# A fused attention and expert kernel: normalising later, values one group later, another tail

## The reference, cut to what matters

```
xn = layernorm(x)
q, k = rope(split(xn @ Wq)), rope(split(xn @ Wk));  v = split(xn @ Wv)
sim = where(causal, q @ k.T * 64**-0.5, -inf)
attn = softmax(sim) @ v;  a = merge(attn) @ Wo + bo
probs = softmax(x @ gate_w.T, over rows);  vals, idx = top_k(probs, 8)
merged = sum over the 8 rows of x[idx] * vals
h = gelu([merged, 1] @ w1);  o = [h, 1] @ w2
out = x + a + scatter_add(o * vals)
```

## Time and profile before

| | us |
|---|---|
| median of three runs | 1408.34 |
| lowest and highest | 1407.0, 1410.91 |
| the profiled execution | 1406.38 |
| its span, first to last instruction | 1404.6 |
| PE busy | 1331.6 (95%) |
| POOL busy | 970.3 (69%) |
| DVE busy | 878.1 (63%) |
| ACT busy | 635.2 (45%) |

### The profile page before, as it was taken

The page is one execution under the profiler, slowest core; times in us unless marked ns, Lnnn a source line. Parts: engine busy times, 40 slices in busy tenths (PEclk is TensorE's granted clock), DMA queues, the critical chain, the costliest instruction groups (busy, mean ns, idle before and its releaser), DMA issues.

```text
span 1404.6 us, 31395 instructions
## 1 busy us (share of the span) xinstructions
PE 1331.6 (95%) x11612; PEld 867.7 (62%) x11612; DVE 878.1 (63%) x1202; ACT 635.2 (45%) x963; POOL 970.3 (69%) x661
## 2 busy tenths in 40 slices
PE   6889999999999999999999999999999999999987
PEld 5556566555655555546676776666656776666655
DVE  5797767666565556556347666666666566666633
ACT  3446565453445334524224434444444344554431
POOL 2666688765566656656566777888778668888842
PEclk9999999999999999999999999999999999999999
DMA  5324333669667866665642222212232221212121
GB/s 177 122 84 145 114 134 116 226 211 320 213 230 244 287 215 221 212 235 171 180 137 81 66 75 65 77 62 77 96 102 91 74 76 55 84 62 77 47 58 57
DMA packets 122752, 188.86 MB, mean 134 GB/s; under 512 B 29616, under 2 KB 57808, under 8 KB 122608
## 3 DMA queue, kind: packets, MB, share of 16 engines
q1 hardware_dynamic: 92176, 112.51, 24.4%
q10 hardware_dynamic: 30384, 74.23, 15.4%
q0 software_dynamic: 48, 0.13, 0.1%
HBM read 130.71 MB, written 22.54 MB: 109 GB/s over the span
## 4 chain that ended last, share of the span: by engine, by line
PE 79%; DMA 7%; DVE 5%; issue 4%; ACT 4%; SPq 1%; POOL 0%; ACTq 0%; DVEq 0%; POOLq 0%
PE t_pO L1490 17%; PE t_pF L1465 11%; PE t_pA L1388 9%; PE t_pB L1388 6%; PE t_pF L1448 6%; DMA t_swap<-t_raw 3%; PE t_pA L1412 3%; PE t_pC L1412 3%; PE t_pA L1393 2%; PE t_pC L1499 2%; PE t_pB L1393 2%; PE t_pB L1540 2%; PE t_pC L1540 2%; PE t_pB L1514 1%; ACT t_PT L812 1%
## 5 line engine op out<-in xcount | busy, mean ns | idle before, releaser
L735 POOL TENSOR_TENSOR t_acc<-t_acc,t_PT 128x1024 f32<-128x1024 f32 (+3 forms) x256 | 437.9, 1711 | 161.8 <-ACT t_PT L812 141.6
L710 POOL TENSOR_TENSOR t_swap<-t_swap,t_sin 128x512 f32<-128x512 f32 x124 | 163.8, 1321 | 198.9 <-DMA t_swap<-t_raw 198.3
L1490 PE MATMUL t_pO<-t_PT,t_V 128*64 128x512 f32 (+3 forms) x1536 | 294.1, 504 | 4.7 <-issue 4.7
L812 ACT ACTIVATE t_PT<-t_pA 128x1024 f32<-128x1024 f32 x192 | 169.7, 884 | 273.1 <-PE t_pA L1400 234.7
L1465 PE MATMUL t_pF<-t_xT,t_wqk 128*128 128x512 f32 x756 | 211.2, 415 | 5.3 <-issue 3.0
L1490 PEld LDWEIGHTS t_pO<-t_PT,t_V 128*64 128x64 f32 x1536 | 94.3, 137 | 145.7 <-issue 129.3
L713 POOL TENSOR_TENSOR t_rot<-t_rot,t_swap 128x512 f32<-128x512 f32 x124 | 174.1, 1404 | 10.8 <-DVE t_rot L1099 1.2
L1465 PEld LDWEIGHTS t_pF<-t_xT,t_wqk 128*128 128x128 f32 x756 | 133.9, 190 | 41.3 <-issue 13.8
L834 ACT ACTIVATE t_raw<-t_pF 128x512 f32<-128x512 f32 x124 | 74.0, 597 | 180.5 <-PE t_pF L1465 136.6
L1089 DVE TENSOR_TENSOR t_LO<-t_rot,t_HI 128x512 fp32r<-128x512 f32 x124 | 147.1, 1186 | 7.5 <-ACT t_HI L844 7.5
L732 POOL TENSOR_TENSOR t_acc<-t_PT 128x768 f32<-128x768 f32 x64 | 142.9, 2232 | 9.6 <-ACT t_PT L812 9.6
(11 more groups left out here) (228 smaller groups left out, 2465.3 us busy)
## 6 DMA issues: line engine op xcount, KB each, us to landing
...
t_OT<-r_s SPq DMA_DIRECT2D x128, 128.0 KB, 2.9
...
```

Source lines behind the costliest of these rows:

```text
L710: pool.tensor_tensor(swap_of(r), swap_of(r), sin[:, c * BANK:(c + 1) * BANK], ALU.mult).then_inc(sin_sem, 1)
L735: pool.tensor_tensor(a[:, :, off:], a[:, :, off:], pt, ALU.add).then_inc(acc_done, 1)
L812: act.activation(PT[:, n % PTS, :, 0:w], bank[:, :, 0:w], ACT.Exp, scale=SCALE).then_inc(exp_done, 1)
L1490: mm = pe.matmul(pO[h * DH:(h + 1) * DH, off:], v, PT[:, n % PTS, h, 0:w], start=(j == 0), stop=(j == 4 * c + 3))
```

## The change

The diff has six parts. First, on TensorE the values of a stage's chunks are multiplied in the next stage, between its maxima and its fill; the experts' transposes come next, still ahead of the fill, and a part right behind the fill. Second, VectorE's `normalise` comes one stage later (s - 4) for all but the last pairs, and in the middle of the stage, behind the maxima and `rope`; the store of batch 0's heads on SP goes one stage later as well, and ScalarE's `copy_out` goes behind the stage's exponentials. Third, the output tiles of batch 0 come one group later, without a special place for the first. Fourth, the statistics of batches 1 to 3 are spread over the stages as before (`spread`), but have one chain, one root and one `moments` for all three, in (1, 1) and (1, 2), and the first unit of batch 1 goes a group later. Fifth, the parts' operands are rounded up to two stages ahead by a table ROUND_AT, into three buffers, and parts use banks pC and pF. Sixth, the last products use four banks in turn.

```diff
@@ -113,7 +113,7 @@
     if MOE + E // GE <= P <= MOE + E // GE + 1:
-        n = (P - MOE - E // GE) * GROUPS + g - 1
+        n = (P - MOE - E // GE) * GROUPS + g - 2
         return [(0, n)] if 0 <= n < NT else []
@@ -125,20 +125,22 @@
+ROUND_AT = {(N - 1, 0): [0], (N - 1, 1): [1], (N - 1, 2): [2, 3], (N - 1, 3): [4], (N - 1, 4): [5], (N - 1, 5): [6], (N, 0): [7]}
+
...
-UNITS_AT = {(0, 5): ("logit", 0), (1, 3): ("x", 1, 0), (1, 4): ("x", 1, 1), (2, 2): ("logit", 1), (2, 3): ("x", 2, 0),
+UNITS_AT = {(0, 5): ("logit", 0), (1, 4): ("x", 1, 0), (1, 5): ("x", 1, 1), (2, 2): ("logit", 1), (2, 3): ("x", 2, 0),
             (2, 4): ("x", 2, 1), (3, 2): ("logit", 2), (3, 3): ("x", 3, 0), (3, 4): ("x", 3, 1), (4, 2): ("logit", 3),
...
 UNIT_STEP = {u: UNIT[u] + sum(DOUBLE[v] < len(DOUBLE) and UNIT[v] < UNIT[u] for v in DOUBLE) for u in UNIT}
-STATISTICS_AT = {(0, 2): [(1, 0)], (0, 3): [(1, 1)], (0, 4): [(2, 0)], (0, 5): [(2, 1), (3, 0)], (1, 0): [(3, 1)]}
-MOMENTS_AT = {(1, 1): 1, (1, 4): 2, (2, 1): 3}
-NORM_AT = {(1, 2): (1, 0), (1, 3): (1, 1), (2, 2): (2, 0), (2, 3): (2, 1), (3, 2): (3, 0), (3, 3): (3, 1)}
+STATISTICS_AT = {(0, 2): [(1, 0)], (0, 3): [(1, 1)], (0, 4): [(2, 0)], (0, 5): [(2, 1)], (1, 0): [(3, 0)], (1, 1): [(3, 1)]}
+NORM_AT = {(1, 3): (1, 0), (1, 4): (1, 1), (2, 2): (2, 0), (2, 3): (2, 1), (3, 2): (3, 0), (3, 3): (3, 1)}
 NORM = {h: n for n, h in enumerate([(0, 0), (0, 1)] + list(NORM_AT.values()))}
...
@@ -418,14 +421,28 @@
+        def rows_of(n):
+            return (slice(1, B), slice(0, NT)) if n == 2 else (0, slice(4 * n, 4 * n + 4))
+
...
-        def next_parts(s):
-            return parts_of(*STAGES[s + 1]) if s + 1 < len(STAGES) else []
+        def normalised_at(s):
+            late = normalise_of(*STAGES[s - 4]) if s >= 4 else None
+            soon = normalise_of(*STAGES[s - 3]) if s >= 3 else None
+            return [n for n in (late,) if n is not None and n < 2 * N - 3] + [n for n in (soon,) if n is not None and n >= 2 * N - 3]
...
+
+        def part_buffers(t):
+            return (oh3[:, :, :], ol3[:, :, :]) if t % 3 == 2 else (oh[:, t % 3, 0:PAIRS - 1, :], ol[:, t % 3, 0:PAIRS - 1, :])
+
+        def part_bank(t):
+            return (pC[:, 1, 0:C], pF[:, 0:C])[t % 2]
+
+        def last_bank(t):
+            return (pC[:, 1, 0:C], pF[:, 0:C], pB[:, 1, 0:C], pA[:, 1, 0:C])[t % 4]
...
@@ -881,20 +898,22 @@
                 act.wait_ge(o_done, 2 * (N - 2) + t // 4 + 1)
-                act.wait_ge(y_mm, (B - 1) * NT - 1 + min(t, 1))
-                if t >= 2:
-                    act.wait_ge(y_part, t - 1)
-                act.activation(oh[:, t % 2, 0:PAIRS - 1, :], OT[:, 0:PAIRS - 1, t * P128:(t + 1) * P128], ACT.Copy).then_inc(oh_done, 1)
+                act.wait_ge(y_mm, (B - 1) * NT)
+                if t == 2:
+                    act.wait_ge(proj_done, len(FILL))
+                if t >= 3:
+                    act.wait_ge(y_part, t - 2)
+                act.activation(part_buffers(t)[0], OT[:, 0:PAIRS - 1, t * P128:(t + 1) * P128], ACT.Copy).then_inc(oh_done, 1)
...
@@ -982,12 +1001,12 @@
                     exp(*chunks[0])
-                if normalise_of(P, g) is not None:
-                    copy_out(normalise_of(P, g))
                 if s and normalise_of(*STAGES[s - 1]) is not None:
...
                     exp(*chunk)
+                if normalise_of(P, g) is not None:
+                    copy_out(normalise_of(P, g))
                 for kind, G, k in slots_of(*STAGES[s - 1]) if s else ():
...
@@ -1038,7 +1056,7 @@
                         round_out(y, t)
-                for t in next_parts(s):
+                for t in ROUND_AT.get((P, g), []):
                     round_part(t)
...
@@ -1322,8 +1345,7 @@
                     invert(n)
-                n = normalise_of(*STAGES[s - 3]) if s >= 3 else None
-                if n is not None and P == N:
+                for n in normalised_at(s):
                     normalise(n)
@@ -1332,12 +1354,15 @@
                     dve.wait_ge(xb_loaded[b - 1], 32)
-                    statistics(b + 1, h)
+                    st = spread(b, h)
+                    if (b, h) == (B - 1, 1):
+                        st.then_inc(stat_done[2], 1)
+                        statistics(2)
                 if (P, g) == (0, 2):
...
                     dve.tensor_tensor(gThl[:, 1, :, :, :], gT[:, :, :, :], gThl[:, 0, :, :, :].bitcast(F32), ALU.subtract).then_inc(g_lo, 1)
-                if (P, g) in MOMENTS_AT:
-                    moments(MOMENTS_AT[P, g] + 1)
+                if (P, g) == (1, 2):
+                    moments(2)
                 if (P, g) == (4, 3):
@@ -1361,11 +1386,8 @@
                         rest(y, t)
-                for t in next_parts(s):
+                for t in ROUND_AT.get((P, g), []):
                     rest_of_part(t)
-                n = normalise_of(*STAGES[s - 3]) if s >= 3 else None
-                if n is not None and P < N:
-                    normalise(n)
@@ -1549,16 +1571,20 @@
-                bank = out_bank(t)
+                bank = part_bank(t)
                 if t >= 2:
...
                     pe.wait_ge(y_done, (B - 1) * NT)
+                    pe.wait_ge(max_done, MAXES[N, 0])
+                    pe.wait_ge(fill_read, len(VFILL))
+                    pe.wait_ge(cos_done, len(ROPE))
                 pe.wait_ge(ol_done, (B - 2) * NT + t + 1)
+                high, low_part = part_buffers(t)
                 a = 0
                 for k in range(PAIRS - 1):
-                    for o, hw in ((oh, 0), (oh, 1), (ol, 0)):
-                        pe.matmul(bank, o[:, t % 2, k, :], woh[:, hw, k, :], start=(a == 0), stop=False)
+                    for o, hw in ((high, 0), (high, 1), (low_part, 0)):
+                        pe.matmul(bank, o[:, k, :], woh[:, hw, k, :], start=(a == 0), stop=False)
                         a += 1
@@ -1566,11 +1592,12 @@
                 pe.wait_ge(y_kept, NT)
-                if t >= 2:
-                    pe.wait_ge(y_done, (B - 1) * NT + t - 1)
+                pe.wait_ge(exp_done, N * len(CHUNKS))
+                if t >= 4:
+                    pe.wait_ge(y_done, (B - 1) * NT + t - 3)
                 pe.wait_ge(wo_loaded, 32)
                 pe.wait_ge(o_done, 2 * (N - 1) + t // 4 + 1)
-                pe.matmul(out_bank(t), OT[:, PAIRS - 1, t * P128:(t + 1) * P128], wlast[:, :],
+                pe.matmul(last_bank(t), OT[:, PAIRS - 1, t * P128:(t + 1) * P128], wlast[:, :],
                           start=True, stop=True).then_inc(y_mm, 1)
@@ -1675,7 +1702,6 @@
                 after_gelu = g == 2 and 0 <= P - MOE < E // GE
-                first_tile = (P, g) == (MOE + E // GE, 1)
                 for m, pieces in enumerate(banks):
@@ -1688,8 +1714,17 @@
                     maximum(pair, MAXES[P, g] + m, (pC, pA)[m % 2], pieces)
+                for chunk in chunks_of(*STAGES[s - 1]) if s else []:
+                    values(*chunk)
+                turns = [x_ for x_ in slots if x_[0] == "turn"]
+                if turns:
+                    pe.wait_ge(exp_done, chunk_index(*chunks[1]) + 1)
+                    pe.wait_ge(max_done, MAXES[P, g] + 1)
+                    slot(*turns[0])
                 if fill_of(P, g) and not after_gelu:
                     fill(fill_of(P, g))
+                for t in parts_of(P, g):
+                    part(t)
                 if chunks:
@@ -1700,23 +1735,14 @@
                     unit(u)
-                for x_ in slots:
-                    if x_[0] == "turn":
-                        slot(*x_)
-                for t in parts_of(P, g):
-                    part(t)
                 for y, t in outputs_of(P, g):
...
                         last(t)
-                    elif not first_tile:
+                    else:
                         output(y, t)
...
                         slot(*x_)
-                for chunk in chunks:
-                    values(*chunk)
-                if first_tile:
-                    output(0, 0)
                 for x_ in slots:
```

57 lines of the change are left out of this document (30 added, 27 removed).

## The result

The changed kernel takes 1451.01 us (median of 4 runs, 1449.48 to 1451.91), the kernel before beside it 1409.21 (4 runs, 1407.0 to 1410.91): ratio 1.0296, 95% interval 1.0278 to 1.0315. I had forecast 1380, with at most 1398 at the upper end of the range. It is slower by 42 us, beyond every case I had; the dearest, the slower D chain, stood at 1437.

The account below looks back on a forecast made before the run. TensorE was taken as the bound, busy 1331.6 of 1404.6 us, so only waits could be gained. Terms -15 + 17 - 13 - 6 - 11 = -28 took 1406.38 to 1378; predicted 1380, eight-in-ten range 1362 to 1398.

Parts of the forecast that it names:

- the slower D chain: Rival: VectorE makes D late by 1 us on average after the transposes, 62 times: 1437 us; chance 0.07.
- 1, later normalising: Pairs 6 to 13: waits worth 28.5 us go, 13.5 us of new waits come: net -15, bounds -28.5 and -4.
- all 28.5 us: Waits in pairs 6 to 13, mostly layer1's in group 0 (17.4 us idle), all taken off as gain.
- the wait moves on: Rival: normalising and late evict delay slot reads in groups 0 and 4 of eight expert pairs: +16, 1396 us; chance 0.19.
- 2, values later: Lost cover: D chain 4.5 us, units of the start 8.4, output tiles 4; together +17, bounds +5 and +35.
- 3, first tile later: Wait for experts' result at 678.44 goes, about 4 us; scattered waits -4; with pairs 23 and 26, -13.
- pairs 23 and 26: Same layer1 wait goes: about 4 us with followers in pair 23, about 1 in pair 26.
- 4, statistics: Start: late maxima from three chains go, 9 us; the one chain left costs +3: net -6, bounds -9 and 0.
- 5, tail: Pair 31's exponential waits covered by values, -5.8; after the last sums -5.1; together -11, bounds -14 and -5.
- the 3 of layer2: Group 2 of pairs 6 to 13: layer2 follows its transposes at once and waits for their copy, 0.4 x 8 = 3 us.
- the squeezes at the slot reads: Pairs 6 to 13: late slot reads cost 0.8 x 8 = 6.5 us in group 0, 0.5 x 8 = 4 in group 4.
- waits of 2 us at the scores behind layer1: Sign that the forecast is wrong: the wait at layer1 has moved on to the next scores.

Follow-up runs that it names:

- n_only: Kernel before with only the heads' output normalised a group later, in the middle of VectorE's stage, and its store a group later: ratio 0.994.
- n_wvs: Kernel before with the later normalising and SP's load of the v weights one group earlier: ratio 0.987.
- v_cover: v_only with the values of pairs 0 to 5 behind the fill, the transpose of the maxima and the unit: ratio 1.034.
- v_only: Kernel before with only the values and the experts' transposes moved as in the change, and copy_out behind the exponentials: ratio 1.019.
- o_only: Change without its values and normalising parts: only statistics chain, later output tiles, parts' operands and last products differ from the kernel before: ratio 0.990.
- v_turn: v_only with the transposes of the maxima ahead of the fill instead of behind it: ratio 1.010.
- after_read: Full change with normalising behind the slot reads for all but the last two pairs: ratio 1.012 to the kernel before.
- vn: Kernel before with the values' new place and the later normalising, without the other four parts: ratio 1.023.

## Why the prediction was wrong, step by step

- **1, later normalising (-15).** This is the step that failed, in its gain and in its price. The waits went; their worth did not. I booked all 28.5 us as free; 15.6 of them lay over the load of the v weights (n_only against n_wvs), and 19.4 were to be had with that load moved. What was late next I named rightly, VectorE's slot read, and sized wrongly: 0.8 us a pair, 6.5 in all; nine waits took 21.5, and behind six of them the clock was lower, which I had put at nothing. The rival "the wait moves on" had the place right, but stopped at 2.2 us: it let only L1075 be long. L1107 and L1090, which stand ahead of it, are held in the same way and at the same time; the trace before had both, 0.68 to 2.72 us (L1089) and 0.15 to 1.27 (L1072). And I put the start at nothing; n_only loses 11 us there.
- **2, values later (+17, bounds +5 and +35).** Alone +1.9%, 26 us: inside the bounds. D cost 0.6 to 0.8 us in a quiet pair, not 0.25; pair 19 after, to hold against the earlier trace rows, is 34.77:

```profile
943.90 0.50 PE L1410 MATMUL t_pA<-t_HI 64*128 64x512 f32 x2
...
974.21 0.33 PE L1410 MATMUL t_pB<-t_HI 64*128 64x128 f32 x2 [0.30 <-issue]
...
978.67 0.50 PE L1410 MATMUL t_pA<-t_HI 64*128 64x512 f32 x2
```

The start cost 19, not 8.4. The reads of pB by the units I had (1.33 us in (3, 5)); ScalarE I had not. It copies logits and normalises x just ahead of the next exponentials. That the values had covered this is my reading; v_cover did not bear it out. In v_only, pair 3, group 3, begun at 200.77, the first exponential starts 2.6 us in, and the maxima wait for bank and exponentials (0.65 and 0.34 us):

```profile
201.01 2.08 ACT L899 ACTIVATE t_xn<-t_xn,t_nbias,t_rstd 128x256 f32<-128x256 f32 x4
203.12 0.38 ACT L861 ACTIVATE t_srow<-t_pC 128x256 f32<-128x256 f32 x1
203.40 1.02 ACT L812 ACTIVATE t_PT<-t_pA 128x1024 f32<-128x1024 f32 x1
```

- **3, first tile later (-13 with pairs 23 and 26).** Pairs 16 to 29 gained 3.7 us by the normalising, near the 5 I had counted there. The tile cost 3.3 instead of giving 4: the change moves SP's loads of its operands with it, which I did not follow through SP's queue. They were issued at 718.43, the tile was due at 719.3:

```profile
718.43 1.00 SPq L699 DMA_DIRECT2D t_os<-o_s  x2
```
```profile
722.80 5.38 PE L1568 MATMUL t_pC<-t_wo,t_os 128*128 128x256 f32 x16 [3.47 <-DMA t_os<-o_s]
```

- **4, statistics (-6).** -4.3 in o_only, from group 2 of pair 0 to pair 5, inside its bounds. Pair 5, 3.6 us longer in the same run, takes most of it back; its wait in (5, 4) stands in v_turn too (2.68 us), which has the old statistics.
- **5, tail (-11).** -8.7 in o_only, inside its bounds. After the last sums 18.5 us, forecast 18.2; pair 31 gave 3.9 and not 5.8, and gave it without the values.
- **The sum.** Sorted by the runs, the forecast was -33.5 for normalising (28.5 and 5 for pairs 23 and 26), +20 for the values (with the 3 of layer2), -25 for the other four parts and +10.5 for the squeezes at the slot reads, which take the first two together: -28. Measured by the ratios they are -8, +26 and -14, and some +37 for the meeting: +42. So of the 71 us of error some 25 lie in the worth of the removed waits, some 27 in the price of the meeting, and the rest in terms 2 to 5. after_read gives back 25 us of the meeting by moving the normalising from ahead of the slot read to behind it. By the profiled spans the meeting is 11 us and the start weighs more.

Of what I said would show it, "waits of 2 us at the scores behind layer1" was the sign, and it came. Open remain the start's share (cover or order, and why normalising alone lengthens pair 1) and what in the full change makes the waits of pairs 6 to 13 longer than in vn.
